# The two low-order products of a logits unit as two 64-row products of TensorE, in both rank stages

## The reference

```
R = adj + I, rows divided by their sums
for n in 0, 1:
    q = Xa @ W1.T @ W2.T          # 4096 x 64
    k = Xa @ W3.T                 # 4096 x 64
    probs = softmax(q @ k.T)      # 4096 x 4096
    A = probs, of each row only the largest that sum to 0.9 kept, divided by the row's sum
    Xf = R @ Xf ; Xa = A @ Xa
    Z += Xf @ U1[n].T + Xa @ U2[n].T
out = layernorm(x + layernorm(x + Z))
```

## Time and profile before

| what | us |
|---|---|
| median of 3 runs | 1665.55 |
| lowest and highest of them | 1661.55, 1665.65 |
| the profiled execution, its own time | 1664.64 |
| its span in the profile | 1662.8 |
| TensorE products busy (PE) | 1531.0 (92%) |
| weight loads busy (PEld) | 887.4 (53%) |
| VectorE busy | 1266.9 (76%) |
| ScalarE busy | 779.7 (47%) |
| GpSimd busy | 244.0 (15%) |
| 16 DMA engines, mean moved | 127 GB/s |

### The profile page before, as it was taken

The page is one execution under the profiler, slowest core; times in us unless marked ns, Lnnn a source line. Parts: engine busy times, 40 slices in busy tenths (PEclk is TensorE's granted clock), DMA queues, the critical chain, the costliest instruction groups (busy, mean ns, idle before and its releaser), DMA issues. The chain is left out here.

```text
span 1662.8 us, 17981 instructions
## 1 busy us (share of the span) xinstructions
PE 1531.0 (92%) x4753; PEld 887.4 (53%) x4753; DVE 1266.9 (76%) x3735; ACT 779.7 (47%) x1237; POOL 244.0 (15%) x283
## 2 busy tenths in 40 slices
PE   7999999979999999998999999998259879899996
PEld 4556556434555555554566666565135445455553
DVE  6788888723677777776799999999868787787664
ACT  4555555412556565564444444444134434445444
POOL 2010210241000000001001111112310221312222
PEclk9999999989999999998999999999569999999998
DMA  7556566644444555555556766672000000000000
GB/s 266 176 154 155 154 171 188 192 180 140 166 173 187 208 208 188 185 202 205 187 155 200 190 182 186 178 177 79 3 2 1 1 8 7 1 7 7 7 7 13
DMA packets 53452, 211.94 MB, mean 127 GB/s; under 512 B 22464, under 2 KB 31232, under 8 KB 32880
## 3 DMA queue, kind: packets, MB, share of 16 engines
q1 hardware_dynamic: 49872, 210.61, 40.7%
q0 software_dynamic: 3488, 0.31, 0.2%
HBM read 206.64 MB, written 4.50 MB: 127 GB/s over the span
## 5 line engine op out<-in xcount | busy, mean ns | idle before, releaser
L1289 ACT ACTIVATE psL<-psL,umax 128x1024 f32<-128x1024 f32 x256 | 278.5, 1088 | 297.1 <-DVE umax L1812 297.0
L1818 DVE MAX8 cand<-psL 128x8 f32<-128x256 f32 (+1 forms) x640 | 372.4, 584 | 57.4 <-PE psL L916 52.1
L915 PE MATMUL psL<-kA,mq 128*128 128x512 f32 x512 | 299.5, 585 | 2.5 <-ACT psL L1289 1.6
L885 PE MATMUL psO<-adj_in,xn 128*128 128x512 f32 x512 | 242.7, 597 | 3.8 <-DMA adj_in<-in_adjT 2.1
L885 PE MATMUL psO<-adj_in,xf 128*128 128x512 f32 x512 | 241.9, 597 | 4.4 <-POOL adj_in L611 4.4
L1097 PE MATMUL psO<-ebuf,xn 128*128 128x512 f32 x512 | 241.5, 593 | 0.5 <-DVE ebuf L2029 0.5
L2029 DVE SCALAR_TENSOR_TENSOR ebuf<-ebuf 128x1024 f32<-128x1024 f32 x128 | 156.7, 1225 | 109.0 <-PE psO L1097 92.2
L1449 ACT ACTIVATE ebuf<-psL 128x1024 f32<-128x1024 f32 x128 | 130.5, 1022 | 187.8 <-PE psL L1143 153.4
L916 PE MATMUL psL<-kB,mq 66*128 66x512 f32 x512 | 203.8, 398 | 0.0
L1398 ACT ACTIVATE ebuf<-psL 128x1024 f32<-128x1024 f32 x128 | 130.9, 1023 | 129.3 <-PE psL L1064 128.9
L1155 PE MATMUL psO<-xf,xa 128*128 128x512 f32 x340 | 167.6, 617 | 5.7 <-DVE xf L2182 5.6
(11 more groups left out here) (341 smaller groups left out, 1962.3 us busy)
## 6 DMA issues: line engine op xcount, KB each, us to landing
adj_in<-in_adjT SPq DMA_DIRECT2D x128, 1024.0 KB, 5.0
adj_in<-in_adj SPq DMA_DIRECT2D x32, 2048.0 KB, 7.6
xaT<-in_xT SPq DMA_DIRECT2D x4, 512.0 KB, 5.4
xa_dram<-xa SPq DMA_DIRECT2D x8, 256.0 KB, 7.8
out<-t SPq DMA_DIRECT2D x8, 256.0 KB, 2.3
list_dram<-ids,place POOLq DMA_INDIRECT x64, 9.3
rel_prob<-cut_dram SPq DMA_DIRECT2D x32, 2.0 KB
cut_dram<-ncut SPq DMA_DIRECT2D x16, 2.0 KB, 8.8
```

The lines of the kernel that those rows point to most:

```text
L885: last = nc.tensor.matmul(psO[:], fs[:, j, :], adj_in[:, r % RING, j % JQ, :], start=(j == 0), stop=(j == JT - 1))
L915: nc.tensor.matmul(o, qA[:, t * P:(t + 1) * P], kA[:, c:c + BI], start=True, stop=False)
L1289: nc.scalar.activation(ps[:], ps[:], ACT.Exp, bias=umax[:, bass.ds(i * UB + k, 1)], scale=1.0, accum_out=usum[:, bass.ds(i * UB + k, 1)]). ...
L1818: last = v.max(cand[:, t % 2, at + c * 8:at + c * 8 + 8], psL[(turn + k) % 3][:, c * WIDE:(c + 1) * WIDE])
```

## The change

The tile kB gets 128 partitions. Partitions 0 to 63 hold k hi as before. In every odd block of 512 columns partitions 64 to 127 hold k hi too: `k_hi` of ScalarE gets a second copy for each unit, of 64 partitions by 512 columns out of PSUM, ahead of the cast to kA. `q_lo` of VectorE writes all 128 partitions of qB, q lo in both halves. A unit is still four products, in a new order: both hi products first (even half, odd half), then the lo product of the even half over partitions 0 to 63 and that of the odd half over partitions 64 to 127, which the instructions place on the upper and the lower 64 rows of the array. They write different PSUM banks. Each of the two adds one to r_l_ps, and VectorE waits for twice the count.

The ones that the later stages need in partitions 64 and 65 of kB are written by VectorE at the start for the even blocks alone (half as much), and by GpSimd for the odd blocks after each rank stage, behind `list_rows` and ahead of its wait for listed. The memset in `first_q_lo` goes; in step 0 a smaller one (2 x 128) is made ahead of the hard rows. The logits of the hard rows and the mix stages keep their products over 128 and 66 rows.

```diff
--- before.py
+++ after.py
@@ -118,7 +118,7 @@
         z = sb("z", [P, T, D])
         xaT = sb("xaT", [D, N])
         kA = sb("kA", [P, N], FP32R)
-        kB = sb("kB", [DA + 2, N], FP32R)
+        kB = sb("kB", [P, N], FP32R)
 
 
         mq = sb("mq", [P, 2, 2, BI], FP32R)
@@ -376,6 +376,8 @@
         OVER_AT = {flow_window(a)[1] - 1: a for a in range(FLOWS)}
         assert len(ROWS_AT) == FLOWS - 1 and len(set(unit // UB for unit in ROWS_AT)) == FLOWS - 1
 
+        kB_odd = kB[:].rearrange("p (b o c) -> p b o c", o=2, c=BI)
+
         def k_bank(u):
 
             return (0, 2, 1, 0)[u]
@@ -685,6 +687,9 @@
                     list_rows(NB - 1)
                     add_x(NB - 1, 0)
                     add_x(NB - 1, 1)
+                if s > 0:
+                    pool.wait_ge(g["r_zx_sb"], 2 * NB)
+                link(nc.gpsimd.memset(kB_odd[DA:DA + 2, :, 1, :].bitcast(FP32), 1.0))
                 pool.wait_ge(g["listed"], 16 * T)
                 pool.wait_ge(g["counted"], 1)
 
@@ -909,13 +914,15 @@
                             if prev is None and k < NU:
                                 pe.wait_ge(g["k_dve"], NU - 1 if k < 2 else NU)
                                 pe.wait_ge(g["k_pool"], max(k + 1, NU - 1) if k < 2 else NU)
-                            for hb in range(2):
-                                c = (u * 2 + hb) * BI
-                                o = psL[(turn + k) % 3][:, hb * BI:(hb + 1) * BI]
-                                nc.tensor.matmul(o, qA[:, t * P:(t + 1) * P], kA[:, c:c + BI], start=True, stop=False)
-                                last = nc.tensor.matmul(o, qB[0:DA + 2, t * P:(t + 1) * P], kB[0:DA + 2, c:c + BI],
-                                                        start=False, stop=True)
-                            last.then_inc(g["r_l_ps"], 1)
+                            tile_ = slice(t * P, (t + 1) * P)
+                            even, odd = psL[(turn + k) % 3][:, 0:BI], psL[(turn + k) % 3][:, BI:UNIT]
+                            c = u * UNIT
+                            nc.tensor.matmul(even, qA[:, tile_], kA[:, c:c + BI], start=True, stop=False)
+                            nc.tensor.matmul(odd, qA[:, tile_], kA[:, c + BI:c + UNIT], start=True, stop=False)
+                            nc.tensor.matmul(even, qB[0:DA, tile_], kB[0:DA, c:c + BI],
+                                             start=False, stop=True).then_inc(g["r_l_ps"], 1)
+                            nc.tensor.matmul(odd, qB[DA:P, tile_], kB[DA:P, c + BI:c + UNIT],
+                                             start=False, stop=True).then_inc(g["r_l_ps"], 1)
                             if prev is not None:
                                 if k == slot(2, UB):
                                     pe.wait_ge(g["r_q_lo2"], i + 1)
@@ -1061,7 +1068,7 @@
                                 j = 2 * u + hb
                                 o = psL[buffer(u, MU)][:, hb * BI:(hb + 1) * BI]
                                 nc.tensor.matmul(o, kA[:, j * P:(j + 1) * P], mqA(i), start=True, stop=False)
-                                last = nc.tensor.matmul(o, kB[:, j * P:(j + 1) * P], mqB(i, slice(0, DA + 2)),
+                                last = nc.tensor.matmul(o, kB[0:DA + 2, j * P:(j + 1) * P], mqB(i, slice(0, DA + 2)),
                                                         start=False, stop=True)
                             last.then_inc(g["m_l_ps"], 1)
 
@@ -1228,6 +1235,7 @@
                 def k_hi(of, u):
 
                     act.wait_ge(of["k_ps"], u + 1)
+                    nc.scalar.copy(kB[DA:P, u * UNIT + BI:(u + 1) * UNIT], psL[k_bank(u)][DA:P, BI:UNIT])
                     nc.scalar.copy(kA[:, u * UNIT:(u + 1) * UNIT], psL[k_bank(u)][:]).then_inc(of["k_act"], 1)
 
                 def q_hi(ps, sb_, i, first=0, last=TB):
@@ -1604,8 +1612,8 @@
             link(v.memset(base[:], 0.0))
             for restart in restarts:
                 v.memset(restart[:, :, 0:1], 0.0)
-            link(v.tensor_copy(kB[DA:DA + 2, :].rearrange("p (b c) -> p b c", c=BI),
-                               t1[DA:DA + 2, :, :].rearrange("p t d -> p (t d)").unsqueeze(1).to_broadcast([2, NB, BI])))
+            link(v.tensor_copy(kB_odd[DA:DA + 2, :, 0, :],
+                               t1[DA:DA + 2, :, :].rearrange("p t d -> p (t d)").unsqueeze(1).to_broadcast([2, NB // 2, BI])))
 
             for s in range(STEPS):
                 g = S[s]
@@ -1625,7 +1633,6 @@
 
                 def first_q_lo(of):
 
-                    link(v.memset(qB[DA:DA + 2, :].bitcast(FP32), 0.0))
                     dve.wait_ge(of["r_q_hi2"], 1)
                     q_lo(of["r_q_hi"], of["r_q_lo"], 0, 0, TB - 1)
                     q_lo(of["r_q_hi"], of["r_q_lo2"], 0, TB - 1, TB)
@@ -1636,7 +1643,7 @@
                 def q_lo(hi, lo, i, first, last):
                     dve.wait_ge(hi, i + 1)
                     c = slice(first * P, last * P)
-                    v.tensor_tensor(qB[0:DA, c], psQ[0:DA, c], qA[0:DA, c].bitcast(FP32), ALU.subtract).then_inc(lo, 1)
+                    v.tensor_tensor(qB[:, c], psQ[:, c], qA[:, c].bitcast(FP32), ALU.subtract).then_inc(lo, 1)
 
                 STEPS_REL, STEPS_CUT, STEPS_PLACE = 4, 20, 9
 
@@ -1804,7 +1811,7 @@
                     for t in range(TB):
                         for u in range(NU):
                             k = t * NU + u
-                            arrived(g["r_l_ps"], i * UB + k + 1)
+                            arrived(g["r_l_ps"], 2 * (i * UB + k) + 2)
                             at = u * WU * 8
 
                             def unit_max():
@@ -1923,6 +1930,7 @@
                         link(v.tensor_tensor(hmid[:], htry, tround[:, 0, 0:1], ALU.mult))
 
                     fresh_chain()
+                    link(v.memset(qB[DA:DA + 2, 0:P].bitcast(FP32), 0.0))
                     prepare(0)
                     with dve.Fori(0, tiles) as c:
                         fresh_chain()
```

## The result

The changed kernel takes 1701.13 us (median of 4 runs, 1700.40 to 1703.84) where the kernel before takes 1665.60 us (4 runs): a ratio of 1.0222, with a 95% interval of 1.0202 to 1.0242. It is 35.5 us slower. The forecast was faster, 1642; the range, 1624 to 1705, held the time by the side of rival D. Of the executions measured with the experiments two were disturbed, one of the kernel before (2015 us) and one of the first experiment (8884 us), and the ratios leave them out.

The account below looks back on a forecast made before the run. TensorE was taken to bound both rank stages, VectorE close behind in step 1. Step 0 -15.6, step 1 -9 and copies +1.8 gave -22.8 us from 1664.64, 1641.8, stated as 1642 for the median; range 1624 to 1705.

Parts of the forecast that it names:

- rival D: Rank stages: the array empties at each change of form, 0.165 us each, giving 1720 us; chance 0.34.
- The bound: Both rank stages hang on TensorE, busy 297.3 of 301 and 369.2 of 375 us, VectorE close behind in step 1.
- The pair: Two lo products of each rank-stage unit: the second starts 0.11 us behind the first, saving 0.122 us a unit.
- rival A: Rank stages: the pair streams side by side, second load ahead, saving 0.229 to 0.233 us a unit; 1627; chance 0.22.
- Going from the full array to half tiles and back: Two changes of form in each rank-stage unit, ahead of and behind the lo pair; taken to cost 0.
- my upper bound: Rank-stage units: 0.165 us for each change of form, and 0.19 more if the load can't go ahead.
- The rule that spoke against the change: Rank stages: going to another tiling mode drains the engine, no price given; the rival built on it had 0.34.
- Steps 0 and 1: Rank stages: shorter units save 15.6 us in step 0 and 9 in step 1, where VectorE's waits cap it at 14.3.
- Copies, q lo, ones: Eight more ScalarE copies of k cost 1.8 us; q lo over 128 partitions nothing; GpSimd's ones 1.9 us, hidden.
- all its signs: Rank stages: distances around the lo pair over 0.3 us, loads beside no product, VectorE waiting over 38 and 14 us.

Follow-up runs that it names:

- the first experiment: The changed kernel with both lo products over 66 rows again, q lo in 64 partitions and the memset back; 1664.73 us, 1.0007 to the kernel before.

## Why the prediction was wrong, point by point

*The bound.* Right. Both rank stages hang on TensorE, and what its unit gets longer came out in both, in step 1 in full and in step 0 for the most part.

*The pair.* Mis-sized, on the safe side. I took 0.122 us from a load that would have to wait for the first lo product; the two loads go at one time, the products start at the same 301.95, and a whole slot comes back (0.236 by the run with both on one tile). In this rival A was right, and so was the Trainium skill ("TensorE: Matmul & The Clock Gate", Part 3) on row tiles that start together; its 4 ns is below what these rows resolve (0.00 to 0.01 us). That page's other half, that loads overlap products only where the row groups differ, the run with both lo products on the same 64 rows contradicts again (303.13).

*Going from the full array to half tiles and back.* **This is the step that failed**: "I take 0, the nearer row", so the unit was to get 0.122 us shorter and got 0.163 longer. The row I leaned on, a 66-row fp32r product followed by a 128-row fp32 one at 0.233 us, was no change of form at all. It changes the data type and the number of rows, but both products stand on the full array, as the run over 66 rows shows. The measured price is 0.20 us for each change, 0.10 of tail and 0.10 of load; my upper bound had 0.165 and 0.19 for these two, and the truth takes part of both. With the pair at 0.233 and two changes at 0.20 the unit comes to +0.17.

*The rule that spoke against the change.* The Trainium skill ("TensorEngine Tiling (Array Packing)", Tiling Modes) says that changing the mode drains the engine while changing the tile does not. The traces agree in the price of both halves: 0.41 to 0.44 from start to start over each change, a plain 0.23 for the second pair inside the form. I gave it 0.34, because the page has no price and my row seemed to speak against it. The row did not bear on it.

*Steps 0 and 1.* -15.6 and -9 were forecast; +16 and +21 came, 42 by the sum. The sum is over by some 6 us, all of it in step 0. There 128 units at 0.163 are 20.9 us; the last logits product comes 18.3 us later (316.76 and 335.05), the last list write 16.0 and the first logits product of step 1 15.2 (775.88 and 791.05). In step 1 the distance from the first to the last logits product then grows by 21.6 us. Much of what step 0 absorbed lies where TensorE had waited for something else. Ahead of a transposition at 222.45 us it waited 0.62 us for ScalarE's copy of z, and does not in the changed kernel; ahead of the fourth unit it waited 1.31 us for ScalarE's exp, and now 1.06. Behind the last unit it waits for an adj transfer, 2.10 us before and 1.36 after, and the eight records behind that wait take 5.40 and 3.70 us; the counting products stand behind them, and the list write behind those:

```profile
326.31 5.40 PE L885 MATMUL psO<-adj_in,xn 128*128 128x512 f32 x8 [2.10 <-DMA adj_in<-in_adjT]
331.54 0.28 PE L979 MATMUL psT<-hard,before 128*128 128x4 f32 x2
```

```profile
344.00 3.70 PE L890 MATMUL psO<-adj_in,xn 128*128 128x512 f32 x8 [1.36 <-DMA adj_in<-in_adjT]
347.54 0.28 PE L986 MATMUL psT<-hard,before 128*128 128x4 f32 x2
```

*Copies, q lo, ones.* The copies: 1.8 us forecast, not measurable; the first logits product is 0.5 us later, where I had 0.6. The copy takes 0.58 us (0.57 estimated). q lo over 128 partitions takes nearly as long as over 64 (419 ns against 410 for the mean of the group). GpSimd's memset takes 1.80 us (1.9 forecast) and is hidden in step 0, where GpSimd still idles 5.88 us behind it, 7.48 before:

```profile
355.30 1.80 POOL L692 MEMSET kB<- 2x2048 f32 x1
362.98 0.60 POOL L701 DMA_DIRECT2D gid<-list_dram  x1 [5.88 <-issue]
```

In step 1 the fetch starts at 1234.28 in place of 1194.31, 3.1 us more than the 36.9 by which its list writes are later, where I had 1.9. VectorE takes up what TensorE makes of it at 1248.11 in place of 1211.24, 36.9 later: hidden, as forecast.

*Rival D.* Its mechanism, place and point of decision (0.061 us a change, or 0.117 with the whole slot won back) hold, and all its signs came: distances over 0.3 us, loads that lie beside no product, longer waits of VectorE. I gave it the same chance as my forecast. Its 1720 came from too small a gain of the pair (0.122, measured 0.23), against a price a little too low (0.165, measured 0.20), and it let nothing be absorbed in step 0. The times of the rivals are counted from the profiled execution and leave out the 0.9 us that 1642 has.

## What to carry to other kernels

Row tiles are not free to enter: on this kernel each change between full-array products and 64-row ones cost 0.20 us, so a visit costs 0.40 us, while each pair inside it saves 0.23. One pair a visit loses. Two save 2 x 0.23 - 0.40 = 0.07 us a visit by this sum, and 7.1 us in all against the same grouping over 66 rows; but the grouping took that back, and against the kernel before they break even at best. By the sum more pairs to a visit would pay better, which no run here tried; look first at whether the buffers behind TensorE allow such a grouping. And when a bound from the trace is "nothing", check that the row chosen is an instance of the very thing that is being added.

## What the runs showed of the hardware that I had not expected

A product over 64 rows can be dearer than the same product over 66. With all else equal (same operands' partitions, same order) the lo products over 66 rows give 1664.7 us and over 64 rows 1761.6 us, which fits a change of form that the shorter one brings (0.33 us from the hi product to it) and the longer one does not (0.23). The two spare rows of zeros in the kernel before, there for the cut of the mix stage, also kept its rank stages out of that.
